# A mixture made block-diagonal for the first step, a reordered opening stage, and three copies in another order

## What is computed

```python
# layer 0, cond: per batch b, a mixture of 8 kernels chosen by attention on the condition
h   = gelu(gelu(cond @ W0 + b0) @ W1 + b1)
att = softmax(h @ W2 + b2)                        # [128, 8]
agg_w = einsum('bk,koi->boi', att, mixw)          # a 32 x 32 matrix per batch
y   = einsum('boi,bih->boh', agg_w, x) + (att @ bias_k)[:, :, None]
# layer 0, ffn: router over 4 experts of rank 16, top 2, softmax gates
x   = x + sum_e gate_e * (y @ A_e.T) @ B_e.T * SCALE
# layer 1, cond: grouped convolution along h (32 channels, 4 groups, 9 taps), plus context and bias
y   = conv(x, convw) + cond @ ctxw.T + fside
# layer 1, ffn: y @ W.T (512 x 512) + LoRA of 8 experts; router with layer norm, top 2, capacity
x   = x + y @ W.T + lora(y)
```

## Time and profile before

| | us |
|---|---|
| median of 3 runs | 313.7 (312.61 to 313.92) |
| profiled execution | 313.72 |
| its span, first to last instruction | 312.0 |
| TensorE busy | 294.0 (94%) |
| VectorE busy | 198.7 (64%) |
| ScalarE busy | 124.6 (40%) |
| GpSimd busy | 97.5 (31%) |
| TensorE's first main product (L1095) starts | 50.97 |
| a repeated step, from gmT's transposes at 104.75 to those at 136.26 | 31.5 |

### The profile page before, as it was taken

The page is one execution under the profiler, slowest core; times in us unless marked ns, Lnnn a source line. Parts: engine busy times, 40 slices in busy tenths (PEclk is TensorE's granted clock), DMA queues, the critical chain, the costliest instruction groups (busy, mean ns, idle before and its releaser), DMA issues.

```text
span 312.0 us, 6202 instructions
## 1 busy us (share of the span) xinstructions
PE 294.0 (94%) x2015; PEld 241.7 (77%) x2015; DVE 198.7 (64%) x503; ACT 124.6 (40%) x261; POOL 97.5 (31%) x127
## 2 busy tenths in 40 slices
PE   7899989989999999999999999999999999898993
PEld 6899867768887788778877887788777877576882
DVE  1469774643749474946494749474958555878784
ACT  4424545424822482248223822382238226111420
POOL 5255215114311421142114211422112316216660
PEclk9999999999999999999999999999999999999998
DMA  6868499796679375947694678466546880004886
GB/s 132 250 131 249 143 239 216 212 184 119 162 225 188 101 196 175 203 101 177 217 179 100 173 226 171 100 171 188 111 100 178 199 165 0 0 2 181 324 326 249
DMA packets 74024, 52.76 MB, mean 169 GB/s; under 512 B 44156, under 2 KB 61004, under 8 KB 74000
## 3 DMA queue, kind: packets, MB, share of 16 engines
q1 hardware_dynamic: 72752, 51.75, 64.9%
q10 hardware_dynamic: 848, 0.55, 0.7%
q0 software_dynamic: 400, 0.16, 0.3%
HBM read 35.67 MB, written 16.78 MB: 168 GB/s over the span
## 4 chain that ended last, share of the span: by engine, by line
PE 71%; DVE 11%; DMA 7%; ACT 4%; issue 4%; SPq 1%; POOL 0%; DVEq 0%; ACTq 0%; POOLq 0%
PE ps_g L1095 13%; PE ps_d L1095 12%; PE ps_a L1056 8%; PE ps_c L1230 7%; PE ps_a L1045 4%; PE ps_t L1246 4%; DMA xg<-x1d 4%; DMA x1d<-xq 3%; PE ps_d L1271 2%; PE ps_v L1068 2%; PE ps_d L1272 2%; ACT xT L555 2%; PE ps_d L1116 1%; PE ps_d L1438 1%; PE ps_d L1442 1%
## 5 line engine op out<-in xcount | busy, mean ns | idle before, releaser
L491 POOL TENSOR_TENSOR o1l<-o,o1h 128x512 fp32r<-128x512 f32 x30 | 39.3, 1311 | 153.3 <-ACT o L616 153.3
L1095 PE MATMUL ps_d<-wt_hi,o1h 128*128 128x336 f32 (+1 forms) x120 | 41.1, 342 | 0.3 <-DVE y_all L931 0.3
L1095 PE MATMUL ps_d<-wt_hi,o1l 128*128 128x336 f32 (+1 forms) x120 | 38.7, 323 | 0.0
L1095 PE MATMUL ps_d<-wt_lo,o1h 128*128 128x336 f32 (+1 forms) x120 | 38.6, 322 | 0.0
L604 ACT ACTIVATE xq<-y_all 128x512 f32 (+1 forms) x29 | 32.6, 1148 | 12.5 <-DVE y_all L931 7.9
L925 DVE TENSOR_TENSOR oT<-ps_c,biasT 128x512 f32<-128x512 f32 x32 | 21.9, 685 | 23.2 <-PE ps_c L1230 23.2
L1095 PE MATMUL ps_g<-wt_hi,o1h 128*128 128x336 f32 x112 | 35.7, 319 | 0.6 <-ACT tmp_all L631 0.4
L1095 PE MATMUL ps_g<-wt_hi,o1l 128*128 128x336 f32 x112 | 35.5, 317 | 0.0
L1230 PE MATMUL ps_c<-xg,cw 96*32 96x512 f32 x256 | 34.1, 605 | 1.4 <-DMA xg<-x1d 1.4
L1095 PE MATMUL ps_g<-wt_lo,o1h 128*128 128x336 f32 x112 | 35.4, 316 | 0.0
L1056 PEld LDWEIGHTS ps_a<-pm,xT 128*128 128x128 f32 x256 | 29.7, 192 | 0.6 <-ACT xT L555 0.5
(11 more groups left out here) (244 smaller groups left out, 590.8 us busy)
## 6 DMA issues: line engine op xcount, KB each, us to landing
xg<-x1d SPq DMA_DIRECT2D x64, 254.0 KB, 4.5
xg<-x1d SPq DMA_DIRECT2D x32, 256.0 KB, 3.5
x1d<-xq SPq DMA_DIRECT2D x30, 256.0 KB, 3.2
xs<-in_x_dram SPq DMA_DIRECT2D x6, 1024.0 KB, 6.0
out_dram<-xT SPq DMA_DIRECT2D x16, 256.0 KB, 2.2
out_dram<-xg SPq DMA_DIRECT2D x16, 256.0 KB, 2.1
y_all<-in_x_dram SPq DMA_DIRECT2D x1, 1024.0 KB, 8.3
y_all<-in_L_ffn_weight_dram SPq DMA_DIRECT2D x1, 1024.0 KB, 6.5
```

The source lines that it names most:

```text
L491: pool.tensor_tensor(lo, o1[t % 2][:, :, :], hi.bitcast(fp32), ALU.subtract).then_inc(s_o1l, 1)
L1095: last = T.matmul(bank[:, 0:columns], a[:, Q - 1 - q, :], w[:, q, first:first + columns], start=(q == 0 and n == 0), stop=(q == Q - 1 and ...
```

## The change

1. The mixture of the first step's 16 batches is no longer taken from the mixture of all batches. attT's first 16 columns are laid out four times with the mask (attD, 64 columns), eight products of 128 rows by 64 columns (L1188 of the new kernel) give it at once, and VectorE instead of GpSimd writes mixbd for step 0 out of PSUM. For this the kernels' rows are dealt out o by o over the four strips, so the four mixw loads read pieces of 32 numbers. The other 112 batches follow in two parts of 16 products with 112 columns, one after step 1's first two x tiles, one after step 0's deltas.
2. TensorE's, ScalarE's and VectorE's streams of the opening are put in another order: the transposes of B between the first two u tiles; the transposes of gw1 behind step 1's x; the weight transposes and splits behind x1 of step 0; x of step 2 among them; u of step 2 in two halves, ahead of and behind the first convolution; u_out(2) ahead of gm_out(1). The 14 fillers that keep_busy issues ahead of the mixture become 10 (3 to 2 and 2 to 1 ahead of the attention, one new behind the first two x tiles, 3 to 0 at the mixture), one new stands ahead of mix(0), and the 8 + 3 + 4 behind it are gone.
3. Loads: the second half of x's first step goes to ScalarE's queue, ffa and ffr from GpSimd's to SP's, B's four ahead of x of step 1, and both x loads of steps 2 and 3 ahead of gw1, gw2, taps and lora_a. B is loaded and split in another column order, which the strided VectorE writes undo.
4. In steps 1 to 5, ScalarE copies xT tiles 0 and 1 ahead of x1_reorder(0) and (1).

The second xT copy has gone ahead of both x1_reorder copies (xq). The core of the diff:

```diff
             for j in range(4):
-                sp.dma_start(wk[C * j:C * j + K0], mixw[:, MO * j:MO * (j + 1)].rearrange("k o i a -> k o (i a)"))\
+                sp.dma_start(wk[C * j:C * j + K0],
+                             mixw.rearrange("k (o j) i a -> j k o (i a)", j=4)[j])\
                   .then_inc(s_ld["mixw"], 16)
-            sp.dma_start(xs_early[0][:, NT // 2:NT, :], x_v[0][:, NT // 2:NT, :]).then_inc(s_xh, 16)
+            sp.dma_start(aw[0:ER0], ffa.rearrange("e r h -> (e r) h")).then_inc(s_ld["aw"], 16)
+            sp.dma_start(aw[ER0:UC], ffr).then_inc(s_ld["aw"], 16)
             sp.dma_start(mbn, row(mixb, 1, BT)).then_inc(s_ld["mixb"], 16)
-            sp.dma_start(xs_early[1], x_v[1]).then_inc(s_x1st, 16)
...
+            sp.dma_start(xs_early[1], x_v[1]).then_inc(s_x1st, 16)
             sp.dma_start(wn, wmain.rearrange("(c p) h -> p c h", p=P)).then_inc(s_ld["w"], 16)
+            for i in range(2):
+                sp.dma_start(xs[i][:, :, :], x_v[2 + i]).then_inc(s_x[i], 16)
...
                     if has(s, 2):
-                        x_transposed(s + 2, (0,))
+                        x_transposed(s + 2, (0, 1))
                     x1_reorder(s + 1, 0)
-                    if has(s, 2):
-                        x_transposed(s + 2, (1,))
                     x1_reorder(s + 1, 1)
...
+            V.tensor_tensor(attD, row(ps_v[:, 0:N0], 1, 4), row(repmask[:, :], 2, N0), ALU.mult).then_inc(s_attD, 1)
             V.tensor_copy(attT, ps_v[:, 0:P]).then_inc(s_ss["attT"], 1)
...
+            dve.wait_ge(s_mp0, 1)
+            V.tensor_tensor(mixbd[:, :, :, :], ps_c[:, :].rearrange("p (o t r) -> p t r o", t=NT, r=BT),
+                            row(row(repmask[:, :], 1, NT), 3, C), ALU.mult).then_inc(s_bd, 1)
...
                 if at_step(s, -1):
 
-                    w_lo(0)
-                    w_lo(1)
                     for t in range(NT):
                         x1_out(0, t, xs_early[0])
...
+                    for j in (1, 3):
+                        dve.wait_ge(s_mps, 2)
+                        V.tensor_copy(mix_home(2, j), mix_part(j)).then_inc(s_msd, 1)
...
-                    w_lo(2)
-                    w_lo(3)
+                    for q in range(Q):
+                        w_lo(q)
                     gates0(1)
...
+            for o in range(MO):
+                last = T.matmul(ps_c[:, o * 4 * N0:(o + 1) * 4 * N0],
+                                wkr[:, o, :, :].rearrange("k r i -> k (r i)"),
+                                attD.rearrange("p j n -> p (j n)"), start=True, stop=True)
+            last.then_inc(s_mp0, 1)
...
                 if at_step(s, -1):
-                    pe.wait_ge(s_v, 1)
-                    keep_busy(8, ps_v)
                     gm_transposed(0)
-                    u_products(1, (2,))
-                    keep_busy(3, ps_v)
+                    u_products(1, (1,))
                     pe.wait_ge(s_gt, 1)
+                    pe.wait_ge(s_msa, 4)
                     delta(0, 0)
                     delta(0, 1)
-                    u_products(1, (3,))
+                    u_products(1, (2,))
                     delta(0, 2)
                     delta(0, 3)
+                    u_products(1, (3,))
+                    pe.wait_ge(s_x1, NT)
+                    mixture(2)
...
-                    keep_busy(4)
-                    u_products(2)
+                    u_products(2, (0, 1))
                     pe.wait_ge(s_cw, 1)
                     pe.wait_ge(s_zero, 4)
                     pe.wait_ge(s_wlo, Q)
                     conv(0, 0)
+                    u_products(2, (2, 3))
```

213 lines of the change are left out of this document (116 added, 97 removed).

## The result

| | before | after |
|---|---|---|
| median, same chip | 313.81 us (6 runs, 312.61 to 314.59) | 317.64 us (6 runs, 316.29 to 319.28) |
| profiled execution | 313.72 | 316.29 |
| its span | 312.0 | 314.6 |
| TensorE's first main product | 50.97 | 57.77 |
| mean granted clock | 0.997 in the profiled execution | 0.973 to 0.984 in the six |

The ratio is 1.0128 (95% interval 1.0091 to 1.0166): slower by 3.8 us. The forecast was 309.7 and its range ended at 312.4, so it was wrong in sign and by 8 us (317.6 less 309.7). Where TensorE's clock falls in some executions of a kernel and not in others, its times spread; ratios here leave out the executions that lie over 1.5% above the kernel's best, medians and ranges hold all.

A forecast was written before the change was run, and what follows sets the result against it. TensorE, running almost without a gap, was taken as the bound, with its xT waits and the opening's chain to shorten. Savings of 3.1 (loop), 0.6 (opening) and 0.3 (gather) sum to 4.0 us: 313.7 to 309.7, range 307.0 to 312.4.

The forecast's parts named there:

- Part 6: Loads: gw1, behind both x loads, lands near 23.8 and is wanted by 24.1, so its wait is hidden.
- rival with 10 in 100: Clock falls to 1.2 GHz at 2.7 us of TensorE idleness ahead of second gmT: 2.5 us longer, 312.2; chance 0.10.
- Part 1: Steps 1 to 5: xT(1) copied ahead of x1_reorder removes five TensorE waits, minus 3.1 us; ends 0 and 3.6.
- Part 2: Opening up to mix(0): 8.5 us from the attention's transpose at 10.4, so mix(0) at 18.9 instead of 22.29.
- late B: Rival in the opening: B's load lands as now, mix(0) 2.3 us later, total 312.0; chance 0.12.
- Part 3: Gate 0, from mix(0) to gmT: 6.9 us instead of 7.8, gmT at 25.8 instead of 30.11.
- nothing stretched: Low end for gate 0: no instruction stretched beside GpSimd's work, 1.4 us less than the 6.9.
- The late case: Rival on loads: gw1 lands at 29.2, gmT and every delta 5.1 us later, total 314.8; chance 0.07.
- Part 5: Gate 1 to first main product: second gmT at 45.0, main at 50.4, minus 0.6 us; ends minus 3.5, plus 2.
- Step 1's gather: TensorE's one wait for a gather in step 1 (1.1 us) shrinks: minus 0.3 us, ends 0 and 1.1.
- Part 4: From gmT to gate 1: 13.4 us against 8.7, so gate 1 starts at 39.2 instead of 38.77.
- the quick opening: Rival: B is early, nothing stretches gate 0 or gate 1 (minus 1.4, minus 1.3), about 307.3; chance 0.13.

The follow-up runs named there:

- The experiment: The kernel before with GpSimd's second block-diagonal product made to wait for gate 0 and without the eight fillers covering that wait: 312.35 us, ratio 0.9971.
- the trimmed one: The kernel before with the loop's new ScalarE order, GpSimd's second block-diagonal product behind gate 0 and without the eight fillers: 309.39 us, ratio 0.9861.

## Why the prediction was wrong, point by point

The step that failed is Part 6, the gw1 load put at "hidden, just" with nothing added for it, together with the clock, which was a rival with 10 in 100 for one gap only. The load landed near 26.95 instead of 23.8. TensorE waited, and its clock fell behind that wait and again behind the second gate's. With gw1 moved ahead and the second gap filled the kernel takes 9.0 us less than the changed one, 308.61 instead of 317.64.

**Part 1, the loop**: right in mechanism, 0.4 us too small. It measured 3.5 alone. A wait cost more than its idle time: in step 2, from gmT's transposes to those of oT, it is 5.46 us in the changed kernel instead of 6.35, 0.89 for a wait of 0.66. Why isn't shown.

**Part 2, up to mix(0)**: 20.79 instead of 18.9. The term that failed is the block-diagonal products, 0.9 us. A u tile of 0.92 us is four products, and eight products were to be made: the row counts two records for each, so 16 records at u's rate are 1.84, and 1.95 was measured. The attention's transpose came at 10.97 instead of 10.4, but that is no error of the sum: the nine other profiles of the same code have it at 9.62 to 10.82. B's load was there in time, without a wait, so late B did not occur.

**Part 3, gate 0**: 6.9 us were forecast; where nothing else waits it takes 5.7 (19.90 to 25.59). I read the stretched 0.92 us of the earlier trace rows as the work of GpSimd's transfers, because their record stands beside it. The experiment shows otherwise, and the end "nothing stretched" was the right one. By the Trainium skill's rule (SBUF — State Buffer, Who interferes with whom), which I weighed and set aside, the trace agrees: beside the issue of transfers none of the two-input instructions is longer than 0.44 us (in the changed kernel too), beside GpSimd's two-input product in gate 1 one is 1.54. How an instruction at 24.09 is held by a product whose record starts at 25.57 stays open. The kernel before without its fillers shows the same, an instruction of 0.93 us at 22.64 and the product's record from 24.14, so GpSimd's records may start late; nothing shows it directly.

**Part 6, loads**: this is where the forecast broke. gw1 was to land near 23.8 and be wanted at 24.1. The DMA rows after:

```profile
0.00:17.40 17.40, 15.56 (x91) 14.33 (x92) 5.80 (x17) 5.90 (x9) 5.99 (x43) 1.00 0.69 192
17.40:24.00 6.60, 6.14 (x76) 5.70 (x76) 2.98 (x15) 1.86 (x5) 4.47 (x9) 1.00 1.00 355
24.00:26.00 2.00, 0.96 (x8) 0.73 (x8) 1.76 (x8) 1.99 (x5) 0.08 (x1) 1.00 1.01 126
```

By 17.4 only 192 times 17.4, 3.3 MB, were moved, not 3.7. The rate behind it, 355 GB/s, was even better than the 327 that I took, and the other 2.5 MB are then through at about 24.3. So the slow front isn't what made gw1 late. The kernel before with its x loads first shows the same: its front moved at the old rate, and gw1 kept TensorE waiting until 26.16 all the same.

```profile
0.00:17.40 17.40, 15.31 (x139) 13.62 (x140) 4.80 (x16) 7.32 (x13) 7.12 (x45) 1.00 0.76 213
17.40:24.00 6.60, 3.67 (x34) 3.53 (x32) 3.08 (x9) 1.11 (x3) 4.82 (x8) 0.93 1.02 305
```

What the sum lacked is the tail: the bytes were through at 24.3, the load landed at 26.95 only. From 24 to 26 the DMA engines are busy to the full at only 126 GB/s. I take it that gw1 shares them with the taps, small pieces that are issued right behind it, from 16.16 on. The trace's packet records fit that: of the packets that start between 24 and 26, 881 have 36 bytes, the nine numbers of a tap row, and 105 have 2048. No run separates it. A reserve of 0.3 us was taken as "hidden, just", and the case was given 7 in 100. Such a margin under a load at the end of 5.8 MB is none. The late case itself was sized about rightly as to the wait: by its rule a landing at 26.95 costs 2.9 us (26.95 less 24.1), and gmT waited 2.4. It missed what stands behind the wait.

**Part 5, the clock**: the rival with 10 in 100 was at work twice. Its price for the second gap was 2.5 us, measured 1.2 in the medians, 1.9 by the ratios and 1.6 in the profile (7.04 us from gmT to main instead of 5.4). But the same mechanism behind the first gap, 3.0 us, wasn't in the list, since the forecast had no gap there. The rivals were added up one at a time, though the late load makes the gap that lowers the clock. Worked through as one case afterwards, with the sizes that the runs gave, it comes out near the profile: the forecast's first main product at 50.4, plus 2.4 for the gmT that waits (28.66, though gate 0 was done at 26.22), plus 3.0, plus 1.6, is 57.4 (measured 57.77). That the forecast's own 50.4 fits so well is in part luck, as the last point says. By the Trainium skill (TensorE: Matmul & The Clock Gate, the table under Why this matters for your kernels), which warns of idle gaps between bursts, the trace agrees in kind; the gaps here, 1.5 to 2.3 us, are smaller than those it warns of.

**Step 1's gather**: minus 0.3 was forecast, plus 1.0 came (its wait is 2.11 us instead of 1.1). With both gaps filled it is 1.1 us again. The lower clock ahead of it is not the whole cause: with only the first gap filled the clock fell behind the second too, and the wait was 0.95. Where the opening is really earlier, as in the trimmed one, it grows as well (2.28). What sets it stays open, and it matters: where it passed 2 us, the stretch from the first main product to the third gmT took 23.8 us when the clock stayed up behind it and 25.3 to 27.6 when it fell, instead of 22.4 to 22.9.

**Part 4 and the sum**: from gmT to gate 1 the mended kernel (gw1 ahead of x, nine fillers) takes 13.3 us, forecast 13.4; its second gmT is at 44.7 (45.0), its first main product at 50.2 (50.4), its time 308.6 (309.7). The walk through the opening was right in sum, with two errors of over a microsecond that cancel (the products 1.05 short, gate 0 1.2 long), which is luck. It was a forecast of a kernel in which gw1 is there and the clock stays. One slip in the rivals changes nothing: the quick opening's terms give 307.0, not 307.3.

## What to carry to other kernels

Whether idle time of TensorE is cheap can't be read from its length alone: ask what the granted clock does behind it, and treat a wait and the slower work behind it as one case with one chance, not as two rivals. Before products that "compute nothing" are cut, or a load is moved behind large ones, look for which wait they cover; here 17 such products are worth 4.2 us. A filler has a price too, when it is still queued as the wait ends: nine ahead of a shorter gate 1 took back all of its 1.36 us. Count products and records apart when a rate is taken from a row, and take a neighbour in time as the cause of a stretched instruction only after it has been moved away.
